# First layer's scores as single-pass products of split queries and keys, with the maximum added by a product of its own

## The reference

```python
q_phi = taylor_feature_map(q @ Wqf)            # 1, x, quadratic terms
k_phi = taylor_feature_map(k @ Wkf)
lin = linear_attention_causal(q_phi, k_phi, v) # weights (q_phi . k_phi), kept where key <= query
scores = jnp.einsum('bqhd,bkhd->bhqk', q, k) * scale
scores = jnp.where(allowed, scores, -jnp.inf)  # key <= query, and key >= query - 64
win = jnp.einsum('bhqk,bkhd->bqhd', softmax(scores), v)
out = jnp.concatenate([lin, win], axis=-1) @ Wout
```

## Time and profile before

| | |
|---|---|
| median of 3 runs | 2100.87 us (2099.36 to 2100.88) |
| the profiled execution | 2098.46 us, span 2096.6 us |
| granted TensorE clock, mean | 0.971 of 2.4 GHz |
| busy share PE, DVE, ACT, POOL | 94%, 62%, 46%, 25% |
| first layer's quads on PE | about 36 to 815 us of the span |
| both layers mixed | about 815 to 985 us |

### The profile page before, as it was taken

One profiled execution on the slowest core, in us unless ns is written; L12 is line 12 of the kernel. 1 busy time (PEld: TensorE's weight loads), 2 busy tenths in 40 slices (PEclk: granted clock), 3 DMA queues, 4 the chain that ended last, 5 costly groups with the idle time before them and its releaser, 6 DMA issues.

```text
span 2096.6 us, 42338 instructions
## 1 busy us (share of the span) xinstructions
PE 1961.9 (94%) x17001; PEld 1428.7 (68%) x17001; DVE 1304.1 (62%) x3139; ACT 957.5 (46%) x1316; POOL 522.1 (25%) x676
## 2 busy tenths in 40 slices
PE   7789999999999988678999999999999999999988
PEld 5455556565656555335878878888788788778887
DVE  4547475767677565647666576566666676675443
ACT  1546565546564554142444444543535434443422
POOL 3334343424334342020121112112202102111111
PEclk8899999999999999788999999999999999999999
DMA  6100212111211013002000000000000010000000
GB/s 184 27 12 25 64 44 65 36 61 47 94 34 64 19 49 136 11 1 81 36 6 24 1 6 24 6 6 19 6 6 18 7 21 4 6 14 6 2 11 9
DMA packets 58035, 67.72 MB, mean 32 GB/s; under 512 B 11928, under 2 KB 48752, under 8 KB 57200
## 3 DMA queue, kind: packets, MB, share of 16 engines
q1 hardware_dynamic: 57008, 64.97, 9.9%
q10 hardware_dynamic: 832, 0.01, 0.0%
HBM read 44.94 MB, written 20.03 MB: 31 GB/s over the span
## 4 chain that ended last, share of the span: by engine, by line
PE 82%; DVE 7%; ACT 5%; issue 4%; POOL 1%; SPq 0%; DMA 0%; ACTq 0%; DVEq 0%; POOLq 0%
PE ps L1899 29%; PE ps L1834 4%; PE ps L1846 4%; PE ps L1020 4%; PE ps L988 4%; PE ps L1803 4%; PE ps L1862 4%; PE ps L1936 3%; PE ps L940 3%; PE ps L1072 3%; PE ps L977 2%; PE ps L998 2%; ACT a_probs L820 2%; DVE ps L673 2%; PE ps L960 2%
## 5 line engine op out<-in xcount | busy, mean ns | idle before, releaser
L1757 ACT ACTIVATE b_acts_exact<-ps,c_s 128x256 f32<-128x256 f32 x256 | 107.5, 471 | 365.6 <-PE ps L1899 365.3
L1899 PE MATMUL ps<-b_acts,b_h2T 128*128 128x256 f32 x2048 | 262.9, 286 | 1.4 <-DVE b_acts L1671 1.4
L1899 PE MATMUL ps<-b_acts,b_h1T 128*128 128x256 f32 x2048 | 260.9, 286 | 1.8 <-POOL b_acts L1528 1.1
L1899 PEld LDWEIGHTS ps<-b_acts,b_h1T 128*128 128x128 f32 x2048 | 249.4, 191 | 18.2 <-issue 14.8
L1899 PEld LDWEIGHTS ps<-b_acts,b_h2T 128*128 128x128 f32 x2048 | 249.9, 191 | 16.0 <-issue 11.1
L440 POOL TENSOR_SCALAR_AFFINE_SELECT a_probs<-a_probs 128x512 f32<-128x512 f32 (+1 forms) x224 | 163.5, 745 | 372.8 <-ACT a_probs L820 214.4
L1520 POOL TENSOR_SCALAR_AFFINE_SELECT b_work<-b_work 128x512 f32<-128x512 f32 x128 | 82.2, 654 | 650.5 <-ACT b_work L1721 650.4
L820 ACT ACTIVATE a_probs<-ps 128x2048 f32<-128x2048 f32 (+1 forms) x96 | 153.0, 1594 | 150.0 <-PE ps L988 148.7
L673 DVE CUSTOM_DVE_ANT_0 ps<-ps,a_band 128x192 f32<-128x192 f32 (+1 forms) x512 | 156.3, 378 | 57.6 <-PE ps L977 57.1
L1592 DVE TENSOR_REDUCE c_nat<-ps 128x4 f32<-128x2048 f32 (+3 forms) x128 | 188.0, 1490 | 3.3
L1721 ACT ACTIVATE b_work<-ps 128x2048 f32<-128x2048 f32 (+1 forms) x96 | 153.2, 1596 | 76.7 <-PE ps L1846 76.3
(11 more groups left out here) (212 smaller groups left out, 3529.0 us busy)
## 6 DMA issues: line engine op xcount, KB each, us to landing
a_raw_next<-in_L_ffn_h_w SPq DMA_DIRECT2D x16, 512.0 KB, 3.9
turned_h<-a_staged SPq DMA_DIRECT2D x32, 256.0 KB, 2.2
a_x<-in_L_attn_x SPq DMA_DIRECT2D x8, 512.0 KB, 4.2
x_mid<-a_x SPq DMA_DIRECT2D x16, 256.0 KB, 2.1
c_x<-x_mid SPq DMA_DIRECT2D x8, 512.0 KB, 4.1
b_h1T<-turned_h SPq DMA_DIRECT2D x1, 4096.0 KB, 16.2
b_h2T<-turned_h SPq DMA_DIRECT2D x1, 4096.0 KB, 12.1
out<-c_x SPq DMA_DIRECT2D x16, 256.0 KB, 2.2
```

The lines of the kernel that those rows point to most:

```text
L1757: ins = nc.scalar.activation(dst[:, j], here[:, j * HALF:(j + 1) * HALF], ACT.Gelu, scale=s12[:, 2 + (name == "h2"), 2 * i + j:2 * i + j + 1])
L1899: ins = nc.tensor.matmul(dst, view(w[:, m, k]), view(src[:, k, i]), start=(k == 0 and i == 0), stop=(k == nk - 1 and i == 1))
```

## The change

- **Split operands.** ScalarE writes the keys rounded to float32r into columns 0 to 15 of each head of `nat`, and VectorE the rest of the keys into columns 16 to 31 (new DVE part of `qk`). The queries are written twice side by side, by ScalarE. So the 32 rows of a head now hold high and low keys (`ksplit`), and the queries twice. The turned queries are split: ScalarE copies the high part (`qhigh`), VectorE subtracts it from what stands in PSUM (`qlow`). The folded queries are split in the same way (`mT`, two parts, now two slots instead of four). `fold` itself has its lower rows made from the rounding rest.
- **Scores.** Each float32 product becomes two float32r products (`qhigh`, `qlow`) that add up in PSUM.
- **The mask** is added in `wm` by a product of the identity with `bandr` (all 128 rows), before the score products; VectorE then takes the maxima with three plain reductions for a quad, instead of 16 combined instructions, and copies them, split in two, into `shift_cols`.
- **The maximum** is added in `win` by a third product for each head and key block, of constant rows (`shift_rows`) with `shifts`, the turned `shift_cols`. `again` now turns `shift_cols`, not the queries, so `nat` isn't cleared for each batch any more. It is cleared once, on GpSimd, before the second layer, and VectorE waits there for it.
- **Keys** are copied by ScalarE instead of VectorE (`tk`).
- **Room in SBUF.** `raw_next` is halved: weights are loaded in 44 halves of 256 KB, each after its own check of the low bits, instead of 22 of 512 KB. Some small tiles move to `kept.x` or into scratch.
- **Order.** `BODY0`, `START` and `TURN` are new lists; `BODY0` has lags of 0 to 2 for most steps of a quad, where it had 1 to 2, and 1 to 3 for the feed-forward part.

```diff
-                once(nc.gpsimd.memset(nat[:], 0.0))
+        once(nc.gpsimd.memset(shift_cols[:], 0.0))
...
 # vector
-            elif name == "tk":
-                nc.vector.tensor_copy(kT[:, b % RING], here).then_inc(free, 1)
+            elif name == "qk":
+                dve.wait_ge(nat_ready, 2 * (NT * b + t + 1))
+                nc.vector.scalar_tensor_tensor(to[:, :, HD:R].bitcast(F32R), here[:, D:2 * D]..., rstd[:, 1, t:t + 1],
+                                               to[:, :, 0:HD], ALU.mult, ALU.subtract).then_inc(free, 1)
+            elif name == "tq":
+                dve.wait_ge(high_ready, b + 1)
+                nc.vector.tensor_tensor(qlow[:, b % RING], here, qhigh[:, b % RING].bitcast(F32), ALU.subtract).then_inc(free, 1)
+            elif name == "fold":
+                dve.wait_ge(folded_high, b + 1)
+                nc.vector.tensor_tensor(mT[:, b % 2, 1], here, mT[:, b % 2, 0].bitcast(F32), ALU.subtract).then_inc(free, 1)
             elif name == "wm":
-                for t, o, first, w in WIN_MAX[step[2]]:
-                    for i in range(4):
-                        ins = nc.vector.tensor_tensor_reduce(part, part, band[:, lo:lo + w], -1.0, -NEG, ALU.add, ALU.min, nat[...])
-                ins.then_inc(free, 1)
+                if step[2] == 0:
+                    nc.vector.tensor_reduce(maxima[:, 0, :].unsqueeze(2), here[:, :, 0:P], AX.X, ALU.max, negate=True)
+                    nc.vector.tensor_reduce(to, here[:, :, P:512]..., AX.X, ALU.max, negate=True).then_inc(free, 1)
+                else:
+                    link(nc.vector.tensor_reduce(maxima[:, 3, :].unsqueeze(2), here[:, :, 0:192], AX.X, ALU.max, negate=True))
+                    dve.sem_inc(free, 1)
+                    link(nc.vector.tensor_copy(shift_cols[:, :, :, 0].bitcast(F32R), maxima[:]))
+                    nc.vector.tensor_tensor(shift_cols[:, :, :, 1].bitcast(F32R), maxima[:], shift_cols[:, :, :, 0], ALU.subtract).then_inc(shift_ready, 1)
...
 # scalar
+                nc.scalar.activation(natk(t)[:, :, 0:HD].bitcast(F32R), here[:, D:2 * D]..., ACT.Copy, scale=rstd[:, 1, t:t + 1])
+                nc.scalar.activation(natq(t)..., here[:, 0:D]....broadcast_to([P, NH, 2, HD]), ACT.Copy, scale=rstd[:, 1, t:t + 1])
+            elif name == "tq":
+                nc.scalar.copy(qhigh[:, b % RING], here).then_inc(high_ready, 1)
+            elif name == "tk":
+                nc.scalar.copy(ksplit[:, b % RING], here).then_inc(free, 1)
...
 # tensor
-            nc.tensor.matmul(here, fold[:], qT[:, step[1] % RING], start=True, stop=True).then_inc(full_sem, 1)
+            nc.tensor.matmul(here, fold[:], qhigh[:, step[1] % RING], start=True, stop=False)
+            nc.tensor.matmul(here, fold[:], qlow[:, step[1] % RING], start=False, stop=True).then_inc(full_sem, 1)
 # window_maxima
+            lo, w = ((0, 512), (P, 192))[j]
+            for i in range(4):
+                nc.tensor.matmul(here[:, i, 0:w], identr[:], bandr[:, lo:lo + w], start=True, stop=False, skip_group_check=True)
             for t, o, first, width in WIN_MAX[j]:
-                for i in range(4):
-                    ins = nc.tensor.matmul(here[:, i, o:o + width], qT[...], kT[...], start=True, stop=True)
+                for part in (qhigh, qlow):
+                    for i in range(4):
+                        ins = nc.tensor.matmul(here[:, i, o:o + width], part[...], ksplit[...], start=False, ...)
 # linear_scores: for part in range(2): ksplit with mT[rows_of(i), n % 2, part, ...]
 # window_scores
+                for part in (qhigh, qlow):
+                    for i in range(4):
+                        nc.tensor.matmul(here[:, i, o:o + w], ksplit[...], part[...], start=(part is qhigh), stop=False)
                 for i in range(4):
-                    ins = nc.tensor.matmul(here[:, i, o:o + w], kT[...], qT[...], start=True, stop=True)
+                    ins = nc.tensor.matmul(here[:, i, o:o + w], shift_rows[rows_of(i)].broadcast_to([R, P]), shifts[rows_of(i), n % 2, to],
+                                           start=False, stop=True)
...
 # second layer, gpsimd, ahead of attention_over: waits for the last again, tk and win
+        nc.gpsimd.memset(nat[:, :, 0], 0.0).then_inc(spare_zero, 1)
+        nc.gpsimd.memset(nat[:, 0:2, 1, :, HD:R], 0.0).then_inc(columns_zero, 1)
+        nc.gpsimd.memset(nat[:, 0:2, 1, :, HD:HD + 1], 1.0).then_inc(spare_zero, 1)
 # second layer, vector
         attention_over(dve)
+        dve.wait_ge(spare_zero, 2)
```

More of the change, by code:

```diff
@@ L390, in run @@
                 if half and b == 3:
+                    sp.wait_ge(rows_placed, 32)
                     for i in range(3):
@@ L455, in run @@
                 power(1, b)
-            elif name == "qk" and b and step[2] == 0:
-                u = fills["again", QUADS * b - 1]
-                pool.wait_ge(filled[u.slot], u.full)
-                nc.gpsimd.memset(nat[:, :, 0, :, HD:HD + 1], 0.0).then_inc(spare_zero, 1)
             elif name == "out" and step[2]:
@@ L1181 @@
[L1181 to L1184 removed]
+0:stats.0 0:norm.0 0:wturn.0.0 0:mod0.0 0:hT.0.0 0:hT.0.1 0:rows.0.0 0:masks.0 0:rms.0 0:wt.0.0 0:qk.0.0 0:qk.0.1 0:qk.0.2 0:qk.0.3 0:v.0.0 0:tq.0
@@ new lines @@
+0:lv.2.0 0:again.3 0:wh.1 0:lin.2.2 0:tq.4 0:tk.4 0:win.2.1 0:wv.2.0 0:fold.4 0:wm.4.0 0:wv.2.1 0:v.1.0 0:lin.3.0 0:lv.2.1 0:lv.2.2 0:wh.2 0:wm.4.1
+0:turn.0.0 0:wt.2.0 0:win.3.0 0:v.1.1 0:lh.2 0:lin.3.1 0:lv.3.0 0:stats.2 0:again.4 0:win.3.1 0:tq.5 0:tk.5 0:win.4.0 0:wv.3.0 0:lv.3.1 0:wv.3.1
+0:lin.3.2 0:wh.3 0:fold.5 0:wm.5.0 0:wv.4.0 0:lv.3.2 0:turn.0.2 0:lh.3 0:wm.5.1 0:turn.0.1 0:win.4.1 0:turn.0.3 0:again.5 0:lin.4.0 0:tq.6 0:out.0.0
+0:lin.4.1 0:out.0.1 0:lin.4.2 0:lv.4.0 0:tk.6 0:wv.4.1 0:lin.5.0 0:fold.6 0:lv.4.1 0:wm.6.0 0:wt.2.1 0:rows.0.1 0:lv.4.2 0:wt.3.0 0:xT.0.0 0:wm.6.1
@@ new lines @@
+0:tk.29 0:lv.28.0 0:wv.27.1 0:win.28.0 0:last.5.0 0:fold.29 0:wm.29.0 0:lv.28.1 0:last.5.1 0:win.28.1 0:turn.6.0 0:lv.28.2 0:wm.29.1 0:turn.6.2
+0:wt.20.0 0:lin.29.0 0:wh.27 0:again.29 0:wv.28.0 0:tq.30 0:lin.29.1 0:turn.6.1 0:turn.6.3 0:tk.30 0:lin.29.2 0:lh.28 0:fold.30 0:wv.28.1 0:wm.30.0
+0:out.6.0 0:wm.30.1 0:out.6.1 0:win.29.0 0:lv.29.0 0:wt.20.1 0:lin.30.0 0:again.30 0:lv.29.1 0:xg.7 0:tq.31 0:win.29.1 0:lv.29.2 0:wh.28 0:lin.30.1
+0:wv.29.0 0:lh.29 0:tk.31 0:win.30.0 0:fold.31 0:lv.30.0 0:xT.6.0 0:wm.31.0 0:wv.29.1 0:wt.21.0 0:wt.21.1 0:lv.30.1 0:wm.31.1 0:lin.30.2 0:wh.29
```

269 lines of the change are left out of this document (147 added, 122 removed).

## The result

The changed kernel is slower by 0.2 to 0.4%: the ratio of the runs is 1.0031, with a 95% interval of 1.002 to 1.0041. The medians of 20 runs each are 2104.16 us, against 2099.85 us before, a difference of 4.3 us; the means, 2105.5 and 2099.3, differ by 6.2 us, since the changed kernel has more long runs. The profiled execution took 2100.53 us (span 2098.5 us), against 2098.46 us before. The runs of the changed kernel spread more than those before (2095.8 to 2116.3 us against 2093.1 to 2101.5), and they do so with TensorE's granted clock: its mean over the span was 0.971 in the shortest and 0.960 in the longest.

The account below looks back on a forecast made before the run. TensorE was taken to set the time in the first layer's quads. From the profiled 2098.5 us, products -0.3 and waits -10 gave 2088; the runs' median lies 2.4 above, so 2090 us, range 2060 to 2130.

Parts of the forecast that it names:

- the term for waits: First layer's quads: half of TensorE's 18.9 us of waits behind L673 comes back, -10 us; ends 0 and -19.
- the new order, taken as even: Both ends of the first layer: the new step order taken as zero, with 8 us put to either side.
- The products: TensorE's `lin`, `win`, `wm` and `fold` per quad: -0.01 us together, -0.3 us in 32 quads; bounds -5 to +22 us.
- the narrow products: Rival: products under 256 columns cost two rounds like float32, +148 us in 32 quads, 2238 us; chance 0.07.
- the covered loads: Rival: TensorE's weight loads hide wholly behind the running round, 33 us less, 2057 us; chance 0.06.
- held banks: Rival: second readers hold the two alternating banks longer, 82 us over 96 fills; at a third reaching TensorE, 2117 us; chance 0.27.
- The loads, priced at nothing: Weights in 44 loads instead of 22: no TensorE wait on weights in the rows, so no cost added.
- VectorE's sum: VectorE's work per quad: 5.57 us before, 5.87 after, +0.3 of some 24.5, taken as covered.
- The set-up: Six short reductions and three `fold` instructions on VectorE, under the loads: no cost placed, about 2 us if that cover failed.

Follow-up runs that it names:

- three places of the order mended: Changed kernel with `tq.3` ahead of `out.1`, the old order of the second layer's part of the turn, and the first weight turn behind `qk`: 2080.69 us.

## Why the prediction was wrong

The forecast was 2090 us, 10 under the kernel before, and the time is 2104: inside the range, on the other side of the kernel before. The step that failed is the term for waits, which took 10 us off for an earlier release of the four-bank room and put nothing in for VectorE's new place in the chain. One subtraction behind a queue on VectorE cost 12.4 us, by the run that moved it. A second term failed beside it: the new order, taken as even, cost 6.5 us where the layers meet.

**The products: right in kind, some us short in sum.** `lin` was to fall from 2.80 to 1.87 us a quad, `fold` by 0.43, `win` and `wm` to rise by 0.20 and 1.15. I take, for each fill, the time from the start of its first record to the start of its last, plus one spacing for the last round. Over the first layer that makes, before and after: `lin` 84 and 51 us (-32, forecast -29.8), `fold` 29 and 19 (-10, forecast -13.8), `win` 48 and 53 (+5, forecast +6.4), `wm` 49 and 91 (+43, forecast +36.8). Together it is about +6 us where -0.3 was forecast, inside -5 to +22. About 5 us of `win`'s 53 are six fills that ran at 1.2 GHz (1.7 to 1.8 us each from first to last start, where 0.96 is usual). A round of 192 or 128 columns starts 0.11 us behind the one before, the price taken was 0.115; the mask's product of 512 columns takes 0.235 (0.215). The rivals of the narrow products and of the covered loads fall with that.

**The waits: the step that failed.** The prediction priced one wait, took half of it back and stopped there; no row gave the half. The relief was larger than forecast, 18.9 us behind L673 against 4.8 behind L704, 14 us in place of 10. But what took its place was seen as a sum over 96 fills (*held banks*) and not looked for in the order list. The list was in the diff: `tk.3` and `fold.3` side by side, `tq.3` six entries behind `out.1`. The earlier trace rows show whom TensorE waits for in the kernel before, not what is queued on VectorE. The two lines on L1030 in the same view, 13.7 us, would have pointed there: they are waits for VectorE at the end of a batch, behind the same `xn` instructions. The new waits behind L691 and L706 are 19.4 us, and the steady loop came out 5.7 us slower than before. With `tq.3` ahead of `out.1` and nothing else moved it came out 6.3 us faster. Five of eight batches of the forecast's 10.3 us are 6.4, so without that place the loop kept what was forecast. In its parts that is luck, since the products cost more and the relief was larger.

**Held banks: right in its outcome, wrong in its size.** Its sign was waits behind the new subtractions or ScalarE's reads that grow beyond 20 us. Those behind the subtractions grew by 19.4 us, those behind ScalarE's reads ahead of `lin` and `win` only from 16.2 to 17.5, so it is just met, and by the subtractions. An eighth of 82 us was to be enough to eat the gain, and 12.4 us is a little more than that. Its mechanism, a bank held for a second reader, is real: when the fold was moved, `lh.0` waited for the bank. But it was priced as evenly spread, and at a third the time was to be 2117. In 26 of 32 quads the second reader came within 0.5 us of the first. The runs show one place in the order, felt in four of eight batches, 12.4 us by itself, without which the change is 0.33% faster than the kernel before.

**The order, taken as even: wrong twice.** The first products came 3.4 us later; undoing that was worth 1.1 us, which the interval doesn't tell from nothing. The order behind the quads lost the 5.6 us of lead and 1 more, 6.5 us by the run that undid it; with that alone the change stands level with the kernel before (0.9991, 0.9976 to 1.0006). Each is under the 8 us that the prediction allowed to either side, and both went the same way. The order of the loop was new too, and no run tries the new products under the old loop order, so what it gave or took apart from `tq.3` is open.

**The loads, priced at nothing: not safe.** "No wait of PE on weights is in the rows" was true of whole pieces and said nothing of halves. The waits of the kernel before hold none for a load of these weights, but in halves the loads cost that kernel 10.0 us. How much of it the changed order hides is open.

**VectorE's sum** was forecast at 0.3 us more a quad, some 10 us in all, and came out 12 us lower, 1292.0 us against 1304.1; 7.6 us of that are the four `xn` instructions of each batch, which met GpSimd's additions less often (31.5 us from 60 to 800 us, 39.1 before). Its mean share of 62% was no cover, since the subtraction was late in its queue, not for want of time. The set-up was not measured by itself.

So the change's arithmetic costs TensorE a few us and frees the four-bank room; with three places of the order mended it runs in 2080.7 us, 0.8% under the kernel before. As it was made, one stop in four of the eight batches and the order where the layers meet took back more than the room gave.

## What to carry to other kernels

When a step gets a second reader on another engine, look in the order list for what that engine has queued ahead of it, and move the step, not its consumer: a consumer moved away leaves the bank held, and the next step waits for it. At a balance of engines, price added work in full (44.8 us for 44 here) and removed work at less than half (16.3 and 19.8 us for 44), until the runs say otherwise. When a queue on one engine is long, ask why its instructions are long before moving what stands behind them: here four of them took 1.7 us together in one batch and some 6 us in four others. Holding GpSimd's additions back from them wasn't tried. A buffer halved to make room for another is an edit of its own: time it alone.

## What the runs showed of the hardware

Behind stops of 4.1 and of 2.2 us TensorE worked for 5.4 us each time at 1.2 GHz before the clock came back. Between 1.5 and 1.9 us the length of the stop alone didn't decide: in the run that took 2080.69 us, 1.8 us (until 473.0) was followed by no fall and 1.5 us (until 665.5) by one. A run's time went with its mean granted clock, 2095.8 us at 0.971 and 2116.3 at 0.960 for the same kernel. I had priced a stop at its length. Single-pass products on 32 rows start 0.11 us apart at 128 and at 192 columns alike at 2.4 GHz, and 0.21 at 1.2 GHz. The `xn` instruction of VectorE (128x256, float32) took 0.40 us where hardly anything of GpSimd ran beside it, 0.5 to 1.2 us beside its shorter instructions, and 2.4 to 2.6 us wherever one of its additions of 128x1024 (some 2.4 us) overlapped it by more than 0.3 us; there it ended 0.15 us after the addition. That holds in all 20 such places of the two traces, before and after; no run moves the additions away.
